# Block-diagonal q laid out in pairs of heads: two-word runs in the score matmuls' moving operand and 512-byte runs in its loads

## The chip, the cores and the metric

The kernel runs on one core of a Trainium2 chip. The metric is the device time of one execution in microseconds (us), lower is better. Engines are named as the profile names them: PE is TensorE (PEld its weight loads), DVE VectorE, ACT ScalarE, POOL GpSimd, SP SyncE, which here only issues DMAs. A "q" behind a name (SPq, ACTq) is that engine's sequencer issuing a DMA.

## What is computed

One decoder layer with three sub-layers, each followed by a residual add and a layer norm, on x of 16 x 256 tokens x 512. The change lies in the first one, a differential attention *across the heads of one token*:

```
q = split(x @ Wq.T) * SCALE      # per token 32 half-heads of 16 dims
k = split(x @ Wk.T)              # the same shape
v = x @ Wv.T                     # per token 16 heads of 32 dims
att  = softmax(q k^T)            # per token
diff = att[:, :16, :16] - lam * att[:, 16:, 16:]
out  = rmsnorm(diff @ v) * (1 - LAM_INIT)
x = layernorm(x + out @ Wo.T + bo)
```

The other two sub-layers are a decayed running sum of ctx*ctx multiplied onto x, and a feed-forward net with ternary weights (512 to 2048 to 512, squared relu). All of it is in float32 precision; large products are made of three (projections) or two (feed-forward) float32r matmuls of a high and a low part.

## The kernel before, in words

The 4096 tokens are cut into 8 blocks of 512 (`NSB`, `SB`). Phase A (`phase_a`, some 455 us) does projections, scores, softmax and the mix with v, in a software pipeline: body(i) of every engine holds the projections of block i, the scores and softmax of block i-1 and the mix of block i-2. Bodies 2 to 5 run in a hardware loop of two bodies per turn. Phase B (`phase_b`) does the rest, block after block; the last block's softmax and mix ("late") are spread over it. Everything is ordered by hand with semaphores; each engine runs its instructions strictly in program order.

In body(i) PE does twelve projection chunks n = 0 to 11 (`project`, L603: 12 matmuls of 512 columns each): 0 to 3 are q, 4 to 7 are k, 8 to 11 are v. Between them it does four bursts of scores of block i-1 (`scores`, L620) behind chunks 0, 1, 6 and 8 (`AT_SCORES`), four bursts of the mix of block i-2 (`mix`, L639) behind chunks 3 to 6 (`AT_MIX`), and four small sums for the ternary weights (`w_sums`, L677).

A token's scores are a product of 16 x 32 by 16 x 32. Eight tokens (`LANES`) share one matmul: lane t keeps its 16 dims on partitions 16t to 16t+15, and the moving operand `qbd` is block-diagonal, zero outside lane t's own slot. The stationary operand is `k2[:, :, g]` (32 columns), and the moving operand is

```
qbd = sb("y", "qbd", [P, LANES, H, G], F32)                       # before, L147
k2[:, :, g], qbd[:, :, :, g].rearrange("p a b -> p (a b)")        # L622
```

so its 128 columns are single words, G = 64 words (256 bytes) apart. Four such matmuls, for four column quarters of the array (32 outputs each), run side by side. Each float32 matmul is two instructions in the trace, so a burst of 32 matmuls shows as x64. The mix has the same construction and the same stride in its stationary operand (`v2[:, :, ...]`, 64 words), but its moving operand `dbd[:, :, n, :]` is eight runs of 16 neighbouring words; a burst of 16 matmuls shows as x32.

How q gets there: ACT copies each projection chunk from the PSUM bank `ps_f` into one of three buffers of `f_sb` (`f_copy`, L902 for q and k, L904 for v), first waiting for the DMA that emptied that buffer, and then issues a DMA into the scratch tensor `q_scr`, `k_scr` or `v_scr` (L909, L911). PE's chunk n waits for ACT's copy of chunk n-2. SP issues the loads: `first_half_load(i)` (k2 and the eight lanes of q for scores bursts 0 and 1), `second_half_load(i)` (the eight lanes of q for bursts 2 and 3), all of them through `q_load` (L388). SP's order in body(i) is: load of x, `dbd_load(i-2)` (L418, eight DMAs that place the softmax difference block-diagonally), `w_write(i-1, 1)`, `w_load(i, 0)`, `second_half_load(i-1)`, `v2_load(i-1)` (L400), `w_write(i, 0)`, `w_load(i, 1)`, `first_half_load(i)`, `o_write(i-2)`.

ACT's order in body(i): `f_copy` 0 to 11; `exps` 0 to 3 (L917, the softmax exponentials of block i-1) behind copies 1, 3, 8 and 11; `w_abs` and `w_sign` (L930, L934) behind copy 2, which wait for the weight load; `mixed` (L923) behind copies 4, 5 and 6 (twice); four `x_upper` (L887) behind copy 7.

DVE's order in body(i): `soft_first` 0 and 1 (L1109 to L1122: transpose out of PSUM, clean, subtract the maximum), `mixed_turn` 0 (L1230), `soft_second` 0 (L1132 on, which waits for the exponentials), `mixed_turn` 1, `square_sum` 0 (L1235), `w_signs`, `soft_second` 1, `mixed_turn` 2, `square_sum` 1, `w_signs`, `mixed_turn` 3, `square_sum` 2 and 3, `rms_seed`, `soft_first` 2, `soft_second` 2, four `x_lower` (L1082), `soft_first` 3, `w_signs`, `soft_second` 3, `diff_turn` (L1221, releases `dbd_load`), `w_signs`.

## Time and profile before

| | |
|---|---|
| runs | 1107.18, 1110.10, 1112.32 us; median 1110.1 us |
| the profiled execution | 1117.94 us, of which the span of its instructions is 1115.8 us |
| PE busy | 1045.4 us (94%), mean granted clock 0.971 |
| DVE, ACT, POOL busy | 868.6, 567.8, 274.4 us |
| DMA | 140.48 MB in 167466 packets, 140368 of them under 512 bytes |
| phase A / the seam / phase B | until about 455 us / 455 to 530 us / from 530 us on |

Busy time counts a matmul from its start to its modelled end; matmuls overlap, so the pace of a burst has to be read from its length and count, not from the mean of one. "PEclk" is the granted clock of PE as a share of 2.4 GHz (0.50 is 1.2 GHz). A bracket behind a line of a timeline, [1.57 <-DMA ...], is the time for which the engine stood idle before it, and what released it.

### The profile page before, as it was taken

The page shows a single profiled execution, that of the slowest core. Times are in us where ns is not written, and L with a number is a line of the kernel's source. Part 1 is how long each engine was busy: PE and PEld are TensorE (multiplying, and loading weights), DVE is VectorE, ACT ScalarE, POOL GpSimd, SP SyncE. Part 2 cuts the span into 40 slices and gives each one's busy share as a digit, 9 for nine tenths or more (in the row PEclk, how much of TensorE's full clock was granted, in tenths as well). Part 3 has the DMA queues.
Part 4 walks back from the last instruction along what each step waited for, and adds up shares of the span by engine and source line. Part 5 has one row for each costly group of instructions (what it writes and reads, how often), then busy time and mean ns, then how long its engine had stood idle before and what let it go on. Part 6 is the DMA issues. An engine that isn't in the chain of part 4 may idle for free.

```text
span 1115.8 us, 19236 instructions
## 1 busy us (share of the span) xinstructions
PE 1045.4 (94%) x6992; PEld 825.1 (74%) x7008; DVE 868.6 (78%) x1326; ACT 567.8 (51%) x866; POOL 274.4 (25%) x272
## 2 busy tenths in 40 slices
PE   6999899899999999686999999999999999999996
PEld 5777667677667776564788888888888888888885
DVE  4478888888889897788798988858958868587455
ACT  5423433334343424323567576665765766656673
POOL 5322252515252525226002003020022320200001
PEclk9999999999999998886999999999999999999998
DMA  7897595958778786978220223411403303110011
GB/s 283 245 225 186 133 242 134 234 150 188 204 162 226 170 249 128 252 189 327 38 76 1 76 76 62 114 43 32 129 1 76 114 1 81 71 38 1 1 38 38
DMA packets 167466, 140.48 MB, mean 126 GB/s; under 512 B 140368, under 2 KB 140880, under 8 KB 161488
## 3 DMA queue, kind: packets, MB, share of 16 engines
q1 hardware_dynamic: 96080, 113.83, 36.9%
q10 hardware_dynamic: 71296, 25.43, 9.3%
q8 instruction: 58, 0.95, 0.4%
q14 instruction: 32, 0.26, 0.1%
HBM read 82.61 MB, written 52.95 MB: 121 GB/s over the span
## 4 chain that ended last, share of the span: by engine, by line
PE 68%; DVE 13%; ACT 5%; DMA 5%; issue 4%; SPq 3%; ACTq 1%; POOL 0%; DVEq 0%; POOLq 0%
PE ps_s L792 20%; PE ps_f L776 19%; PE ps_f L603 12%; PE ps_o L728 7%; PE ps_s L620 5%; SPq L418 2%; DMA w_in<-in_fc_turned 2%; DVE row_sum L1132 1%; PE ps_o L639 1%; DMA w_scr<-w_in 1%; DVE o_sb L1230 1%; ACT f_sb L902 1%; DVE st L1145 1%; DMA w_raw<-in_qkvo 1%; PE ps_t L762 1%
## 5 line engine op out<-in xcount | busy, mean ns | idle before, releaser
L776 PE MATMUL ps_f<-x2h,w 128*128 128x512 f32 x512 | 205.0, 400 | 2.7 <-DVE x2l L1374 2.7
L776 PE MATMUL ps_f<-x2l,w 128*128 128x512 f32 x512 | 201.1, 393 | 0.0
L792 PE MATMUL ps_s<-w,hh 128*128 128x512 f32 x500 | 196.6, 393 | 0.0
L792 PE MATMUL ps_s<-w,hl 128*128 128x512 f32 x500 | 194.9, 390 | 0.0
L1382 DVE TENSOR_TENSOR hl<-h_sb,hh 128x512 fp32r<-128x512 f32 x128 | 90.0, 703 | 100.7 <-ACT hh L1004 100.6
L603 PE MATMUL ps_f<-xth,wh 128*128 128x512 f32 x376 | 158.2, 421 | 8.7 <-ACT f_sb L902 5.6
L603 PE MATMUL ps_f<-xtl,wh 128*128 128x512 f32 x376 | 149.6, 398 | 0.0
L603 PE MATMUL ps_f<-xth,wl 128*128 128x512 f32 x376 | 149.4, 397 | 0.0
L620 PE MATMUL ps_s<-qbd,k 128*32 128x128 f32 x2048 | 124.9, 411 | 11.7 <-DMA qbd<-q_scr 11.7
L994 ACT ACTIVATE r_sb<-ps_f 128x512 f32<-128x512 f32 x128 | 75.7, 591 | 104.7 <-PE ps_f L776 104.5
L620 PEld LDWEIGHTS ps_s<-qbd,k 128*32 128x32 f32 x2048 | 82.6, 147 | 49.1 <-issue 12.1
L776 PEld LDWEIGHTS ps_f<-x2h,w 128*128 128x128 f32 x512 | 97.3, 190 | 23.2 <-issue 3.6
L776 PEld LDWEIGHTS ps_f<-x2l,w 128*128 128x128 f32 x512 | 97.2, 190 | 19.4
L1574 POOL TENSOR_TENSOR w_in<-w_in,gscale 128x512 f32<-128x512 f32 x32 | 52.8, 1651 | 231.7 <-DVE gscale L1257 216.7
L792 PEld LDWEIGHTS ps_s<-w,hh 128*128 128x128 f32 x500 | 93.9, 188 | 19.1
L792 PEld LDWEIGHTS ps_s<-w,hl 128*128 128x128 f32 x500 | 94.0, 188 | 18.9
L1603 POOL TENSOR_TENSOR ln_rs<-ln_x,neg_half 128x4 f32<-128x4 f32 x23 | 23.2, 1009 | 338.0 <-DVE ln_x L1329 338.0
L1012 ACT ACTIVATE h_sq<-h_sb 128x512 f32<-128x512 f32 x128 | 79.4, 620 | 52.3 <-DVE h_acc L1393 52.2
L603 PEld LDWEIGHTS ps_f<-xth,wh 128*128 128x128 f32 x376 | 72.4, 192 | 34.8 <-issue 15.9
L902 ACT ACTIVATE f_sb<-ps_f 128x512 f32<-128x512 f32 x64 | 38.3, 599 | 112.8 <-PE ps_f L603 102.5
L603 PEld LDWEIGHTS ps_f<-xth,wl 128*128 128x128 f32 x376 | 72.4, 193 | 16.2
L1004 ACT ACTIVATE hh<-h_sb 128x512 fp32r<-128x512 f32 x128 | 81.0, 633 | 4.1
(158 smaller groups left out, 1832.1 us busy)
## 6 DMA issues: line engine op xcount, KB each, us to landing
q_scr<-f_sb ACTq DMA_DIRECT2D x32, 256.0 KB, 4.3
k_scr<-f_sb ACTq DMA_DIRECT2D x32, 256.0 KB, 2.6
w_scr<-w_in SPq DMA_DIRECT2D x16, 512.0 KB, 4.0
k<-k_scr SPq DMA_DIRECT2D x8, 1024.0 KB, 8.8
qbd<-q_scr SPq DMA_DIRECT2D x128, 64.0 KB, 4.6
v_scr<-f_sb ACTq DMA_DIRECT2D x32, 256.0 KB, 6.1
cx<-in_ctx_turned SPq DMA_DIRECT2D x8, 1024.0 KB, 4.9
xb<-in_x SPq DMA_DIRECT2D x8, 1024.0 KB, 5.2
```

What stands on the lines that cost most here:

```text
L603: last = nc.tensor.matmul(ps_f[:, n % 2, :], w[:, n // 4, k, cols], xx[:, par, k, :], start=(k == 0 and xx is xth and w is wh), stop=(k == ...
L620: last = nc.tensor.matmul(ps_s[32 * j:32 * (j + 1), 2 * (c % 2) + gq // 4, (gq % 4) * P:(gq % 4 + 1) * P], k2[:, :, g], qbd[:, :, :, g].re ...
L728: last = nc.tensor.matmul(proj_bank(i, t), a[:, k, rows], w[:, k, :], start=(k == 0 and w is woh and a is oth), stop=(k == KC - 1 and a is ...
L776: last = nc.tensor.matmul(ps_f[:, j % 2, :], w1[:, j // 2, k, (j % 2) * P:(j % 2 + 1) * P], xx[:, k, :], start=(k == 0 and xx is x2h), sto ...
L792: last = nc.tensor.matmul(ps_s[:, t, :], a[:, j % 4, t * P:(t + 1) * P], w2[:, j, :], start=(j == 0 and a is hh), stop=(j == HC - 1 and a ...
L902: nc.scalar.activation(f_sb[:, n % 3, :], ps_f[:, n % 2, :], ACT.Copy).then_inc(f_ev, 1)
L994: nc.scalar.activation(r_sb[:], ps_f[:, j % 2, :], ACT.Relu).then_inc(r_done, 1)
L1004: nc.scalar.activation(hh[:, j % 4, :], h_sb[:, j % 4, :], ACT.Copy).then_inc(hh_done, 1)
L1012: nc.scalar.activation(h_sq[:, j % 2, :], h_sb[:, j % 4, :], ACT.Square).then_inc(hq_done, 1)
L1382: nc.vector.tensor_tensor(hl[:, j % 4, :], h_sb[:, j % 4, :], hh[:, j % 4, :].bitcast(F32), ALU.subtract).then_inc(hl_done, 1)
L1574: nc.gpsimd.tensor_tensor(w_in[:, half(r)], w_in[:, half(r)], gscale[:, half(r)], ALU.mult).then_inc(wt_md, 1)
L1603: nc.gpsimd.tensor_tensor(y[:], x[:], neg_half[:], ALU.pow).then_inc(signal, 1)
```

## The change

The columns of Wq are reordered on the host, so that chunks 0 and 1 hold the first half-head set with even and odd heads and chunks 2 and 3 the second. ACT writes an even chunk into every even word of a new buffer `q_sb` and an odd chunk into every odd word, so that two heads of one token are neighbours. One DMA per pair of chunks writes 4096 bytes per partition into `q_scr` (16 such DMAs of 512 KB in place of 32 of 256 KB), and `q_load` reads it back in runs of 128 words, 512 bytes (the eight DMAs of 64 KB each stay). `qbd` keeps its size and becomes [P, LANES, H/2, G, 2]: the score matmul's moving operand is now 64 pairs of neighbouring words, 512 bytes apart. `f_sb` gets a fourth buffer (q_sb lies over it), with the waits rewritten for that. `o_sq` now lies over `dt`, and `r_sb` and three regions move in SBUF. Number and sizes of matmuls, ACT and DVE instructions stay.

```
-    q_scr = nc.dram_tensor("q_scr", [NSB, D, SB], F32, kind="Internal").ap()
+    q_scr = nc.dram_tensor("q_scr", [NSB, 2, P, LANES, 2 * G], F32, kind="Internal").ap()
+        q_sb = sb("x", "q_sb", [P, 2, SB, 2], F32)
-        f_sb = sb("x", "f_sb", [P, 3, SB], F32)
+        f_sb = sb("x", "f_sb", [P, 4, SB], F32)
-        qbd = sb("y", "qbd", [P, LANES, H, G], F32)
+        qbd = sb("y", "qbd", [P, LANES, H // 2, G, 2], F32)
...
             def q_load(i, s):
                 for t in range(LANES):
-                    sp.dma_start(qbd[H * t:H * (t + 1), lane_slot(t), :, :],
-                                 q_scr[i, s * 256:(s + 1) * 256, t * G:(t + 1) * G]
-                                 .rearrange("(d a) g -> d a g", a=H)).then_inc(qbd_ld, 16)
+                    sp.dma_start(qbd[H * t:H * (t + 1), lane_slot(t), :, :, :].rearrange("p a g r -> p a (g r)"),
+                                 q_scr[i, s, :, t, :].rearrange("(d a) n -> d a n", a=H // 2)).then_inc(qbd_ld, 16)
...
-                                            k2[:, :, g], qbd[:, :, :, g].rearrange("p a b -> p (a b)"),
+                                            k2[:, :, g], qbd[:, :, :, g, :].rearrange("p l a r -> p (l a) r"),
...
             def f_copy(i, n):
                 act.wait_ge(f_ps, at(i, 12, n + 1))
-                if n >= 3 or later(i):
-                    act.wait_ge(f_wr[n % 3], at(i, 64, 16 * (n // 3)))
+                if n < 4 and n % 2 == 0 and later(i):
+                    act.wait_ge(f_wr[n], at(i, 48, 0))
+                    act.wait_ge(f_wr[n + 1], at(i, 32, 0))
+                if 4 <= n < 8 and n % 2 == 0:
+                    act.wait_ge(f_wr[n % 4], at(i, 48, 16))
+                if n >= 8:
+                    act.wait_ge(f_wr[n % 4], at(i, 48 - 16 * (n % 2), 32 - 16 * (n % 2)))
...
+                if n < 4:
+                    nc.scalar.activation(q_sb[:, n // 2, :, n % 2], ps_f[:, n % 2, :], ACT.Copy).then_inc(f_ev, 1)
...
+                if n in (0, 2):
+                    return
                 act.wait_ge(f_ev, at(i, 12, n + 1))
                 if n < 4:
-                    act.dma_start(q_scr[i, rows, :], f_sb[:, n % 3, :]).then_inc(f_wr[n % 3], 16)
+                    act.dma_start(q_scr[i, n // 2].rearrange("p t n -> p (t n)"),
+                                  q_sb[:, n // 2, :, :].rearrange("p n r -> p (n r)")).then_inc(f_wr[n - 1], 16)
```

## Rows read from the trace of the kernel before

**Rows 1.** Busy time by stretch: us, each engine's busy (instructions), PEclk, DMA, GB/s.
```profile
core 0: us, PE busy (x) PEld busy (x) DVE busy (x) ACT busy (x) POOL busy (x), PEclk, DMA share, GB/s
254.20:313.40 59.20, 54.54 (x538) 40.74 (x534) 52.15 (x62) 22.43 (x29) 22.84 (x25) 1.00 0.78 190
530.00:1116.00 586.00, 572.18 (x2755) 471.48 (x2753) 437.31 (x802) 374.04 (x612) 76.69 (x72) 0.99 0.19 53
```

**Rows 2.** The chain that ended last: shares of the span by line.
```profile
by line: PE ps_s L792 19.9%; PE ps_f L776 19.4%; PE ps_f L603 11.6%; PE ps_o L728 6.5%; PE ps_s L620 5.4%; issue 4.4%; SPq L418 2.2%; DMA w_in<-in_fc_turned 1.7%; DVE row_sum L1132 1.5%; PE ps_o L639 1.3%; DMA w_scr<-w_in 1.2%; DVE o_sb L12
```

**Rows 3.** PE's timeline, 258 to 320 us: start, length, instruction, count, [idle before].
```profile
280.57 3.92 PE L620 MATMUL ps_s<-qbd,k 128*32 128x128 f32 x64 [1.57 <-DMA qbd<-q_scr]
...
296.89 1.11 PE L639 MATMUL ps_o<-dbd,v 128*32 128x128 f32 x32
...
312.28 1.11 PE L639 MATMUL ps_o<-dbd,v 128*32 128x128 f32 x32 [1.47 <-DVE o_sb L1230]
```

**Rows 4.** One instruction of the scores and of the mix: ns minimum/median/maximum, first and last.
```profile
L620 PE MATMUL ps_s<-qbd,k x2048: 393/413/440, 51.4 to 498.9; 128*32 128x128 f32 x187
...
L639 PE MATMUL ps_o<-dbd,v x896: 272/273/429, 117.7 to 475.5; 128*32 128x128 f32 x180
```

**Rows 5.** PE's timeline around the seam, and the granted clock there.
```profile
457.95 7.61 PE L620 MATMUL ps_s<-qbd,k 128*32 128x128 f32 x128 [4.03 <-DMA qbd<-q_scr]
466.07 1.11 PE L639 MATMUL ps_o<-dbd,v 128*32 128x128 f32 x32 [0.52 <-DMA dbd<-dt]
...
473.99 1.94 PE L639 MATMUL ps_o<-dbd,v 128*32 128x128 f32 x32 [1.29 <-DVE o_sb L1230]
...
459.00:462.00 3.00, 3.00 (x60) 2.17 (x56) 2.74 (x4) 0.00 (x0) 0.79 (x1) 0.75 0.32 73
474.00:477.00 3.00, 1.93 (x32) 1.35 (x32) 3.00 (x3) 2.66 (x5) 0.00 (x0) 0.50 1.03 317
```

**Rows 6.** The chain from 193 to 314 us: start, length, what.
```profile
254.22 3.69 PE ps_s L620 x57
...
266.63 1.23 DVE row_sum L1132
...
284.59 1.26 DVE dt L1221
...
292.63 2.85 DMA w_scr<-w_in
...
295.71 4.16 DMA w_in<-in_fc_turned
```

**Rows 7.** Who waited for whom (us in total, times, longest); DVE's timeline at 443 us.
```profile
DVE row_sum L1132 <- ACT sc L917: 13.9, 8, 2.3
...
DVE st L1109 <- PE ps_s L620: 11.4, 5, 4.0
...
443.52 1.22 DVE L1132 TENSOR_REDUCE row_sum<-sc 128x32 f32<-128x1024 f32 x1 [1.25 <-ACT sc L917]
```

**Rows 8.** The chain from 30 to 136 us: the first q load, four projection chunks.
```profile
45.61 5.76 DMA qbd<-q_scr
...
62.12 11.38 PE ps_f L603 x48
```

**Rows 9.** ACT's timeline in the first pipelined block.
```profile
66.18 1.06 ACT L930 ACTIVATE w_b<-w_in 128x1024 bf16<-128x1024 f32 x1 [0.47 <-DMA w_in<-in_fc_turned]
...
68.24 0.57 ACT L902 ACTIVATE f_sb<-ps_f 128x512 f32<-128x512 f32 x1
```

**Rows 10.** ACT's groups by shape: busy, mean ns of one, idle before.
```profile
L923 ACT ACTIVATE o_sq<-o_sb 128x512 f32<-128x512 f32 x28 | 31.0, 1106 | 36.8 <-DVE o_ms L1235 17.9 <-DVE o_sb L1230 12.3 <-ACT f_sb L902 6.6
L904 ACT ACTIVATE f_sb<-ps_f 128x512 f32<-128x512 f32 x32 | 19.2, 601 | 43.5 <-PE ps_f L603 42.4 <-DMA v_scr<-f_sb 1.1
```

**Rows 11.** A pause of PE with a lower clock behind it: timeline, and stretch.
```profile
339.76 3.92 PE L620 MATMUL ps_s<-qbd,k 128*32 128x128 f32 x64 [1.57 <-DMA qbd<-q_scr]
...
342.00:345.00 3.00, 3.00 (x36) 2.10 (x29) 2.77 (x4) 0.00 (x0) 0.14 (x1) 0.60 0.99 381
```

More of the change, by code:

```diff
@@ L91, in program @@
         base = (nc.sbuf_base + 31) // 32 * 32
-        region = {"x": base, "y": base + 90 * 1024, "z": base + 122 * 1024,
-                  "c": base + 154 * 1024, "s": base + 202 * 1024}
+        region = {"x": base, "y": base + 92 * 1024, "z": base + 124 * 1024,
+                  "c": base + 156 * 1024, "s": base + 202 * 1024}
         spot = dict(region)
@@ L153, in program @@
         p1 = sb("c", "p1", [P, G, H], F32)
+        o_sb = sb("c", "o_sb", [P, HD, G], F32)
+        spot_c = spot["c"]
+        o_sq = sb("c", "o_sq", [P, SB], F32)
+        spot["c"] = spot_c
         dt = sb("c", "dt", [P, G, H], F32)
-        o_sb = sb("c", "o_sb", [P, HD, G], F32)
-        o_sq = sb("c", "o_sq", [P, SB], F32)
         w_b = sb("c", "w_b", [P, 2 * D], BF16)
@@ L218, in program @@
         f_ps, f_ev = sem("f_ps"), sem("f_ev")
-        f_wr = [sem(f"f_wr{n}") for n in range(3)]
+        f_wr = [sem(f"f_wr{n}") for n in range(4)]
         qbd_ld = sem("qbd_ld")
@@ L380, in hold, with q_written, k_written, v_written @@
                     sp.sem_inc(passed, 1)
-            def f_written(i, chunks):
-                return [(f_wr[n % 3], at(i, 64, 16 * (n // 3 + 1))) for n in chunks]
+            def q_written(i, s):
+                return [(f_wr[2 * s], at(i, 48, 16))]
+            def k_written(i):
+                return [(f_wr[n], at(i, 48 - 16 * (n % 2), 32 - 16 * (n % 2))) for n in range(4)]
+            def v_written(i):
+                return [(f_wr[n], at(i, 48 - 16 * (n % 2), 48 - 16 * (n % 2))) for n in range(4)]
             def q_load(i, s):
                 for t in range(LANES):
-                    sp.dma_start(qbd[H * t:H * (t + 1), lane_slot(t), :, :],
-                                 q_scr[i, s * 256:(s + 1) * 256, t * G:(t + 1) * G]
-                                 .rearrange("(d a) g -> d a g", a=H)).then_inc(qbd_ld, 16)
+                    sp.dma_start(qbd[H * t:H * (t + 1), lane_slot(t), :, :, :].rearrange("p a g r -> p a (g r)"),
+                                 q_scr[i, s, :, t, :].rearrange("(d a) n -> d a n", a=H // 2)).then_inc(qbd_ld, 16)
             def k2_load(i):
@@ L979, in x2_upper @@
                 if t == 0 and not later(i):
-                    for n in range(3):
-                        act.wait_ge(f_wr[n], at(NSB, 64, 0))
+                    for n in range(4):
+                        act.wait_ge(f_wr[n], at(NSB, 48 - 16 * (n % 2), 0))
                     act.wait_ge(wt_wr, at(NSB, 32, 0))
@@ L1656, in turned, with q_columns, k_columns @@
     return a.reshape(NSB, SB, KC, P).transpose(0, 3, 2, 1)
-def head_columns(w, order):
-    return w.T.reshape(D, H, QD, 2).transpose(0, *order).reshape(D, D)
+def q_columns(w):
+    return w.T.reshape(D, H // 2, 2, QD, 2).transpose(0, 4, 2, 3, 1).reshape(D, D)
+def k_columns(w):
+    return w.T.reshape(D, H, QD, 2).transpose(0, 2, 3, 1).reshape(D, D)
 def layouts(inputs):
-    qkvo = np.stack([head_columns(inputs["L0_attn_Wq"], (3, 2, 1)), head_columns(inputs["L0_attn_Wk"], (2, 3, 1)),
+    qkvo = np.stack([q_columns(inputs["L0_attn_Wq"]), k_columns(inputs["L0_attn_Wk"]),
                      inputs["L0_attn_Wv"].T, inputs["L0_attn_Wo"].T])
```

22 lines of the change are left out of this document (12 added, 10 removed).

## The prediction, made before the changed kernel had run

> **What bounds the kernel now.** I read the busy time by stretch first. From 530 us to the end, more than half of the span, PE is busy 572 of 586 us and the change touches nothing there [rows 1]. In phase A it is less clear: a block takes about 59 us, PE is busy 54.5 and DVE 52.2 of 59.2 [rows 1]. So two engines are nearly full, and what is taken from one may leave the other. The chain of work that ended last gives the score bursts 5.4% of the span, 60.3 us or 16 of the 32 bursts [rows 2]. That is the most the matmul part of the change can touch. The same chain within a block then shows what closes the round: score burst 2 (254.22), projection, the exponentials, DVE's row_sum (266.63), DVE's dt (284.59), eight DMA issues of `dbd_load`, the write of ternary weights (292.63), the next weight load (295.71), ACT, DVE, and burst 2 again at 313.39 [rows 6]. Only one of the block's four bursts is in that round; the other three sit beside DVE work.
>
> **The change, part by part.**
>
> *The score matmuls.* A burst of 64 instructions takes 3.92 us [rows 3]; less the last one's own 0.41 [rows 4] and over 63 intervals that is 55.7 ns each. The mix has the same 128 columns, the same 32 output columns and the same stride of its stationary operand, but runs of 16 words in the moving one: 1.11 us for 32 [rows 3], less 0.27 [rows 4], over 31: 27 ns. So reading single words 256 bytes apart costs half the rate. The clock confirms it: in the seam two bursts in a row take 7.61 us, (7.61 - 0.41) / 127 = 56.7 ns, though the granted clock was down to 0.75 there, while a mix burst at 0.50 takes 1.94 us, (1.94 - 0.43) / 31 = 49 ns [rows 4, 5]. The scores keep one pace at both levels of the clock (1.2 and 2.4 GHz), and it is about the mix's pace at the lower one; the mix follows the clock. A fetch of one word at a time at a fixed rate would explain both, and two words per fetch would just feed the upper level. No row shows runs of two words. The bounds are 55.7 ns (no gain) and 27 ns; I take 27, since the factor to be closed is two and the run length is two. A burst then takes 2.05 us in place of 3.92, 1.87 less at full clock and nothing at half clock.
> The Trainium skill ("Advanced Engine Details and Errata", SBUF Cachelines) says that SBUF is read in lines of 16 bytes and that at least two hits on a line are needed to absorb the access latency. By that rule two words get the full rate, as above, and the sum is this one; the trace agrees with it for one word (55.7 ns) and for sixteen (27), and no row tries two.
>
> *What of it counts.* Twice 1.87 before burst 2 of the first block, where PE alone is in the chain. But ACT cannot do copy 3 before the weight load lands: it starts at 68.24, behind two operations that began at 66.18 when the load came [rows 9]. Four chunks took 11.38 us, 2.85 each, and ended at 73.50 [rows 8]. Projection 5 waits for that copy: 68.24 + 0.6 + 2.85 = 71.7 against 73.5, so 1.8 is gained there, not 3.7; burst 2's own 1.87 then reaches DVE, which was waiting for it. Sum 3.7.
> From then on the round of rows 6 decides. DVE's row_sum waited 13.9 us in 8 cases for the exponentials [rows 7], because ACT took projection copies 7 and 8 first, and these waited for PE. PE 1.87 earlier frees ACT, but an exponential takes 1.1 itself and can't begin before DVE's own subtraction; where it did begin at once the wait was 1.25 [rows 7]. So seven waits fall to 1.25: 13.4 - 8.8 = 4.6. The eighth (0.53, last block) gives 0.5. DVE also waited 11.4 us in 5 cases directly for scores [rows 7]; 8.6 of it lies in the start already counted, 2.8 in one block after a long pause of PE; 0 to 2.8, I take 1.1, since the weight load is late next. These make 6.2.
> The other bursts are faster beside DVE work: nothing. PE will arrive earlier at burst 0 and wait longer for the q load.
>
> *The loads.* Half of the packets of the q loads go; their eight issues per half stay. The load is in the chain once, 5.76 us at the start [rows 8]; between nothing and a third of it (q is a third of the bytes landing with k2): 0 to 1.9, I take 0.5. Elsewhere PE waits 1.57 for it without being the bound [rows 3].
> The Trainium skill ("DMA: Bandwidth & Descriptors", Why small descriptors are slow) gives a 256-byte descriptor 11 cycles, which makes a 512-byte one 19 by the same formula: 14% less per byte, near the low end; no row here separates the q loads' packets.
>
> *The writes.* 32 DMAs of 256 KB become 16 of 512 KB. The one behind copy 2 was issued beside the weight load of rows 6 (4.16 us) and is now gone; 256 KB at the 317 GB/s seen in a full stretch [rows 5] are 0.8 us. 0 to 0.8 in each of six blocks; I take 0.3: 1.8. The pair's write lands later, but the q loads wait for the k chunks, written afterwards. The new waits are as loose as the old: copy 4 waits for a write issued behind copy 1, three chunks back as before. SP's extra waits are for semaphores long reached. Behind ACT's wait at copy 2 stand `w_abs` and the rest of ACT; it is for v writes of the block before, as it was.
>
> *ACT's strided copies.* Output in every second word, 32 times. Nearest rows: 601 ns for a copy with a permuted output in 16-word runs, and 1106 ns for a square that reads words 256 bytes apart [rows 10]. I take 600, since two neighbouring hits in 16 bytes are the closer case, so nothing. At 1106 only copy 3 lies in the round (weights, copy 3, exponential, copy 4, square, DVE): 0.5 x 6 = 3.0 lost.
>
> *What comes late next.* In the seam PE had scores to do from 457.95 to 465.6; now it is through about 2 to 3.7 us earlier and pauses before the mix at 466.07, which runs in the chain at full clock (1.11), where the third and fourth take 1.94 at half clock [rows 5]. I count two at the lower clock: 2 x 0.83 = 1.7 lost.
>
> Sum: 3.7 + 4.6 + 0.5 + 1.1 + 0.5 + 1.8 - 1.7 = 10.5 us. Against the profiled execution's own 1117.9 (span 1115.8 and 2.1 around it) that gives 1107.4; the median of the runs is 7.8 lower, 1110.1, and the saving, which is phase A's and not a share of the whole, is the same there: **1099.6 us**.
>
> **The rivals.**
>
> *Two words aren't enough.* The matmuls stay at 56 ns, the change doesn't do its main work, and the loads and writes remain: 0.5 + 1.8, or less 3.0 if the copies are slow. 1107.8 to 1110.8, say 1108. For it: no row has such runs. Against it: the fixed pace at both clocks, which looks like one word per fetch. 21%.
>
> *The chain's share in full.* PE was the real bound throughout, and other waits follow it down: 60.3 us of bursts in the chain times 1.87 / 3.92 are 28.8 us less, 1081. Against it: DVE's 52.2 busy of 59.2, plus the waits for exponentials that can't go. 13%, with anything beyond 1088.
>
> *The clock takes it back (slower).* PE now has 10 us or more of pauses per block. The pause before the fourth mix is 1.47 us [rows 3], and a pause of 1.57 elsewhere was followed by a clock of 0.60 [rows 11], one of 1.57 at 280.57 by none. If pauses before that mix grow or add up so that the clock is 0.50 behind it, burst 2 gains nothing and projections 7 and 8, 2.85 us each at full clock [rows 8], take twice that: 5.7 us late in a round that has no slack for it. In all five steady blocks: 28.5 lost and the 4.6 not won; with the rest of the sum, 1110.1 - 5.9 + 28.5 = 1132.7. Each such block costs 5.7 and 0.7 of the gain, so one or two leave a small gain or none, and from three on it is slower. Against it: nothing before that mix gets faster, since no score burst lies between chunk 2 and it. The skill's "TensorE: Matmul & The Clock Gate" (HAM oscillation) warns of just this, full clock lost again after waits; the trace agrees after the pause in rows 11 and not after the one in rows 3. 10%.
>
> **How the numbers follow.** The forecast's own case, 1092 to 1106, has 56%. The four cases make 100%. The range reaches to the "not enough" case and its slow copies above, and to half of the full share below: 1086 to 1113; outside it are most of the full-share case and the clock case, and some of the main one. A measurement of this kernel can tell about 0.5%, 5.6 us, from no change. Faster: nearly all of the main case, all of the full share: 68%. Same: "not enough", and edges of the main and the clock case: 23%. Slower: 9%.
>
> **What the profile of the changed kernel would show.** The score burst: x64 in about 2.05 us in full clock (3.9 would mean that pairs don't help; 3.0 that they help by half). ACT's q copies at 0.60. The row_sum wait of burst 2 at about 1.25. A block of about 58 us with PE busy near 50. The pause before burst 0, behind the q load, at 5 us in place of 1.57, with a lower clock behind it that harms nobody. In the seam mix bursts of 1.94. Wrong would be the forecast if blocks fell to 55 us (then PE was the bound), or if the clock were at 0.5 in the projections behind burst 2.

## The result, and the profile after

The changed kernel takes 1107.1 us against 1110.2 us for the kernel before on the same chip (20 runs each): ratio 0.9971, 95% interval 0.996 to 0.9981, so 2.1 to 4.4 us less, 3.2 by the ratio. The forecast was 10.5 less. Direction right, size three times too large. The profiled execution has a span of 1106.2 us; single executions scatter by some 5 us, so its 9.6 us to the profile of before are not the result.

First the page of the changed kernel, the lines that answer to the table shown of before:

```profile
span 1106.2 us, 19193 instructions
PE 1017.5 (92%) x7008; PEld 824.6 (75%) x7008; DVE 876.5 (79%) x1326; ACT 570.4 (52%) x866; POOL 278.9 (25%) x272
...
PEclk9999999999999989686999999999999999999998
...
DMA packets 148777, 140.47 MB, mean 127 GB/s; under 512 B 107344, under 2 KB 124240, under 8 KB 142800
```

PE has 28 us less to do and the span of this profile is down by 9.6: most of what PE saved turned into waits of PE. Note DVE: its work is the same, instruction for instruction, and it is busy 7.9 us longer. That is the first sign of where the rest went. The same in one block (us, busy of each engine with its count, clock, DMA share, GB/s):

```profile
133.00:192.00 59.00, 50.97 (x533) 40.50 (x532) 53.59 (x61) 22.11 (x29) 23.02 (x24) 0.97 0.72 187
```

PE 50.97 against 54.54 in [rows 1], DVE 53.59 against 52.15.

Next the score matmuls: PE's timeline, and the instruction's own time (ns minimum/median/maximum):

```profile
315.76 2.57 PE L632 MATMUL ps_s<-qbd,k 128*32 128x128 f32 x64
```

```profile
L632 PE MATMUL ps_s<-qbd,k x2048: 297/312/441, 48.1 to 489.0; 128*32 128x128 f32 x187
```

Where [rows 3] had 3.92 us there are now 2.57 to 2.63: (2.57 - 0.31) / 63 = 35.9 ns each, where 27 were forecast. Of the 1.87 us forecast for a burst, 1.3 came.

The waits that answer to [rows 7] (who waited for whom, us in total, times, longest), and two that grew:

```profile
DVE row_sum L1153 <- ACT sc L938: 9.1, 7, 2.3
...
ACT w_b L951 <- DMA w_in<-in_proj_turned: 15.0, 6, 3.1
...
PE ps_f L615 <- ACT q_sb L918: 7.8, 8, 2.0
```

The wait for the exponentials fell from 13.9 us in 8 cases to 9.1 in 7: 1.13 us in each but the first. That step went as forecast. ACT now waits in six blocks for the other half of the weight load (15.0 us in all; 0.6 and 1.7 in the two executions of the kernel before), and PE waits a little longer for the copies of q (7.8 us against 5.6). What stands behind row_sum in the same block did not go as forecast. Here are DVE and POOL from chunk 2's subtraction (L1122, L1143 in the changed kernel) on, first in a second execution of the kernel before (start, length, instruction, [idle before]):

```profile
201.29 1.32 DVE L1122 SCALAR_TENSOR_TENSOR sc<-sc,row_max 128x1024 f32<-128x1024 f32 x1
203.68 2.62 POOL L1565 TENSOR_TENSOR o_sb<-o_sb,o_rs 128x512 f32<-128x512 f32 x2
204.65 1.22 DVE L1132 TENSOR_REDUCE row_sum<-sc 128x32 f32<-128x1024 f32 x1 [2.04 <-ACT sc L917]
205.90 0.35 DVE L1135 RECIPROCAL row_inv<-row_sum 128x32 f32<-128x32 f32 x1
206.29 0.75 DVE L1145 SCALAR_TENSOR_TENSOR st<-sc,lam,row_inv 128x512 f32<-128x512 f32 x1
```

and then in the changed kernel:

```profile
138.96 1.60 DVE L1143 SCALAR_TENSOR_TENSOR sc<-sc,row_max 128x1024 f32<-128x1024 f32 x1
141.69 1.22 DVE L1153 TENSOR_REDUCE row_sum<-sc 128x32 f32<-128x1024 f32 x1 [1.12 <-ACT sc L938]
141.81 2.54 POOL L1586 TENSOR_TENSOR o_sb<-o_sb,o_rs 128x512 f32<-128x512 f32 x2 [0.26 <-POOL o_rs L1579]
142.94 0.35 DVE L1156 RECIPROCAL row_inv<-row_sum 128x32 f32<-128x32 f32 x1
143.33 1.56 DVE L1166 SCALAR_TENSOR_TENSOR st<-sc,lam,row_inv 128x512 f32<-128x512 f32 x1
```

POOL's two multiplies (the rms scaling of the block before) started 0.97 us ahead of row_sum and ended at 206.30, just as DVE's `scalar_tensor_tensor` began at 206.29: they ran in DVE's wait and beside a reduction. In the changed kernel the multiplies start 0.12 us behind row_sum, and the same DVE instruction takes 1.56 us in place of 0.75. Counted from burst 2 and block for block, row_sum comes 0.6 us sooner and the multiplies 0.3 us later (at 7.39 to 7.59 us in place of 7.13 to 7.33), since POOL's small steps ahead of them take longer. The subtraction ahead of the exponential has grown too, from 1.32 to 1.60. The subtraction of chunk 3 meets the second pair of multiplies in both kernels: 2.17 to 2.21 us in the kernel before, 2.17 to 2.51 in the changed one.

The kernel before shows the meeting once itself, in its last block, where row_sum had waited only 1.25 us. From its first execution, block 2 and the last one:

```profile
205.24 2.62 POOL L1565 TENSOR_TENSOR o_sb<-o_sb,o_rs 128x512 f32<-128x512 f32 x2
207.86 0.75 DVE L1145 SCALAR_TENSOR_TENSOR st<-sc,lam,row_inv 128x512 f32<-128x512 f32 x1
...
443.37 2.61 POOL L1565 TENSOR_TENSOR o_sb<-o_sb,o_rs 128x512 f32<-128x512 f32 x2
445.17 1.36 DVE L1145 SCALAR_TENSOR_TENSOR st<-sc,lam,row_inv 128x512 f32<-128x512 f32 x1
```

Where the time went, by stretch, in us. All numbers are read from DVE's and PE's timelines; "burst 2" is DVE's transpose of burst 2. Of the columns of numbers the third and fourth are means of five blocks, the fifth of six.

| execution | first burst to burst 2, first block | six blocks | burst 2 to row_sum | row_sum to dt | dt to the next burst 2 | last burst 2 to the end |
|---|---|---|---|---|---|---|
| before, first and second | 29.08, 29.27 | 355.7, 354.1 | 8.02, 8.04 | 17.83, 17.82 | 33.6, 33.3 | 679.6, 680.2 |
| after, first and second | 27.71, 25.46 | 352.2, 351.4 | 7.46, 7.41 | 18.81, 18.81 | 32.6, 32.5 | 678.1, 679.2 |

In the two middle columns, where the forecast had its largest term, a block got 0.6 us shorter and 1.0 longer. These two repeat to 0.05 us. The others hold landings of DMAs and scatter, so that the two pairs differ by 9.6 and 6.7 us in all, where the runs give 3.2.

### The profile page after: what moved, and what is told of

Read it like the earlier page. It is cut to its first block, busy times and chain, and to the rows that moved or that the text cites. A ratio compares the mean times of both kernels' runs of the same rounds, so it can differ in the third digit from the quotient of the medians.

```text
span 1106.2 us, 19193 instructions
## 1 busy us (share of the span) xinstructions
PE 1017.5 (92%) x7008; PEld 824.6 (75%) x7008; DVE 876.5 (79%) x1326; ACT 570.4 (52%) x866; POOL 278.9 (25%) x272
## 4 chain that ended last, share of the span: by engine, by line
PE 54%; DVE 24%; ACT 6%; issue 6%; DMA 4%; SPq 3%; ACTq 2%; POOL 0%; DVEq 0%; POOLq 0%
PE ps_s L804 20%; PE ps_f L788 20%; PE ps_o L740 6%; SPq L430 3%; PE ps_f L615 3%; DVE row_sum L1153 2%; DMA w_in<-in_fc_turned 2%; DVE st L1166 2%; DVE sc L1136 2%; DVE row_max L1139 2%; DVE st L1130 2%; DMA w_scr<-w_in 2%; ACT o_sq L944 1%; ACTq L932 1%; DVE gscale L1278 1%
## 5 line engine op out<-in xcount | busy, mean ns | idle before, releaser
L1595 POOL TENSOR_TENSOR w_in<-w_in,gscale 128x512 f32<-128x512 f32 x32 | 56.0, 1751 | 220.0 <-DVE gscale L1278 206.2
L632 PE MATMUL ps_s<-qbd,k 128*32 128x128 f32 x2048 | 84.3, 322 | 7.5 <-DMA qbd<-q_scr 7.5
L632 PEld LDWEIGHTS ps_s<-qbd,k 128*32 128x32 f32 x2048 | 74.9, 139 | 16.9 <-DMA qbd<-q_scr 8.8
L615 PEld LDWEIGHTS ps_f<-xtl,wh 128*128 128x128 f32 x376 | 73.4, 195 | 14.3
```

Source lines behind the costliest of these rows:

```text
L615: last = nc.tensor.matmul(ps_f[:, n % 2, :], w[:, n // 4, k, cols], xx[:, par, k, :], start=(k == 0 and xx is xth and w is wh), stop=(k == ...
L632: last = nc.tensor.matmul(ps_s[32 * j:32 * (j + 1), 2 * (c % 2) + gq // 4, (gq % 4) * P:(gq % 4 + 1) * P], k2[:, :, g], qbd[:, :, :, g, :] ...
L1595: nc.gpsimd.tensor_tensor(w_in[:, half(r)], w_in[:, half(r)], gscale[:, half(r)], ALU.mult).then_inc(wt_md, 1)
```

## The experiments

Each ratio is to runs of the kernel before on the same chip, with its 95% interval; "us" is the ratio's difference times 1111. Bursts are those of the first block.

### The two kernels once more

> The kernel before once more, for a second profile of it. The first one took 1117.9 us while the runs lie at 1110.2, and the gap between the two profiles (spans 1115.8 and 1106.2, 9.6 us) is three times the measured gain of 3.1. Theory A (the first profile was an unusual execution): this one is at 1108 to 1113, with steady blocks of 57.5 to 59.5 us, without the load of 6.07 us and the PE stall that made two blocks 60.5 long. Theory B (profiling costs this kernel 7 us): it is at 1117 again with the same blocks.

> The changed kernel once more. Its blocks should repeat: about 58.5 us each, score bursts of 2.6 us, DVE's L1166 behind the exponentials of burst 2 at about 1.56 us, where L1145 of the kernel before takes 0.75, if that is the regular collision with POOL's multiplies that I take it for; at 0.75 in half of the blocks if it is chance.

Measured: 1113.7 and 1107.0 us, spans 1111.5 and 1104.9, so theory A within a microsecond. In both executions of the kernel before the `scalar_tensor_tensor` of chunk 2 takes 0.75 to 0.89 us in every block but the last, which has 1.36; in the changed kernel it takes 1.38 to 1.56 from the second block on (in the second execution from the third). So the pattern belongs to the kernels, not to one execution.

### Pair reads alone, and words in place of pairs

```
-  k2[:, :, g], qbd[:, :, :, g].rearrange("p a b -> p (a b)"),              # before
+  k2[:, :, g], qbd[:, :, 0:16:2, 2 * (g // 2):2 * (g // 2) + 2],            # e1
-  ... qbd[:, :, :, g, :].rearrange("p l a r -> p (l a) r"),                 # after
+  ... qbd[:, :, :, g, :].rearrange("p l a r -> p l r a"),                   # e2
```

> The kernel before with only the score matmuls' moving operand changed: 64 pairs of neighbouring words, 512 bytes apart, from the old layout, so it multiplies wrong columns of q; loads, copies and writes are those of before. Theory 1 (the matmuls' reads are the whole effect, and DVE's round decides): bursts of 2.6 us and a time like the changed kernel's, 1106 to 1108.5. Theory 2 (matmuls bring more, and the strided copies of 0.69 us and the larger writes take it back): 1101 to 1104.

> The changed kernel with the moving operand read in an order that makes every word single again (512 bytes apart; heads come out permuted), so only loads, copies, writes and buffers are changed. Bursts of 3.9 us. Theory 1: 1109.5 to 1112, no difference from before. Theory 2: 1112 to 1116, the copies and writes cost.

Measured: e1 0.9938 (0.9918 to 0.9958), 6.9 us less, with bursts of 2.23 us. e2 1.0102 (1.008 to 1.0124), 11.3 us more, with bursts of 4.90 us:

```profile
47.56 4.90 PE L632 MATMUL ps_s<-qbd,k 128*32 128x128 f32 x64
```

Neither fits its theories: the time of e1 is in the range of theory 2, but its bursts are not the 2.6 us that both took for given, and e2 is above every range. Pairs alone gain twice what the whole change does; and single words cost 70 ns ((4.90 - 0.48) / 63) where the kernel before paid 55.7. So at the same run length the new layout is slower than the old, and something in the addresses beside the run length sets the pace. In both kernels four matmuls, for four column quarters ("tiles"), run side by side and read columns g that are 16 apart: 64 bytes in the kernel before and in e1, 128 in the changed kernel and in e2. (Against the kernel before, e2 also doubles the step within one matmul, from 256 to 512 bytes, so for single words the two are not separated. For pairs they are: the step is 512 bytes in all of the kernels with pairs.)

### Is it the rest of the change, or the addresses?

```
-  qbd[:, :, :, g, :]                                            # after
+  qbd[:, :, :, g // 2, :]                                       # e10
-  nc.scalar.activation(q_sb[:, n // 2, :, n % 2], ps_f...       # after
+  nc.scalar.activation(<q_sb[:, n // 2] as 1024 words>[(n % 2) * SB:(n % 2 + 1) * SB], ps_f...   # e7
```

> The changed kernel, but matmul g reads the pairs of column g // 2 instead of g (so the scores are made from other columns of q). Every matmul still reads 64 pairs of words 512 B apart; only the distance between the four column tiles' reads falls from 128 to 64 B, as it is in the kernel before with pair reads (bursts 2.23 us there, 2.6 us in the changed kernel). Theory 'address': the 2.6 us come from where the pairs lie; bursts fall to 2.2 to 2.3 us, the waits of chunk 2's row_sum stay at 1.13 us, the first block and the blocks' lengths hardly move, and the time is 0 to 1.5 us under the changed kernel (3 to 4.6 us under the kernel before). Theory 'rest of the change': bursts stay at 2.6 us and the time stays 3.1 us under the kernel before.

> The changed kernel, but each of the four copies of q writes 512 words in one run, each chunk in its own half of the paired buffer (so q's words are in another order). Theory 'strided copies': they cost 694 ns against 599 ns, 28 of them, and TensorE's projection waits for them; the copies fall to 600 ns, the waits of the projection for q_sb fall from 7.8 us by 1 to 2 us, and the time is 1.5 to 3 us under the changed kernel (4.6 to 6 us under the kernel before). Theory 'the copies are covered': they fall to 600 ns and the time stays within 0.7 us of the changed kernel.

Measured: e10 0.9931 (0.9908 to 0.9953), 7.7 less, bursts 2.23 us: with the addresses of e1 the changed kernel is as fast as e1 (0.8 us apart, give or take 3.3), so its copies, writes and loads together cost and bring nothing that shows. The theory 'address' was right on the bursts, and the time fell by more than the 3 to 4.6 us that I had put to it. e7 0.9972 (0.9957 to 0.9986), 3.1 less, the changed kernel's own time. ACT's group of q copies (busy, mean ns of one, idle before), first changed kernel, then e7:

```profile
L918 ACT ACTIVATE q_sb<-ps_f 128x512 f32<-128x512 f32 x32 | 22.1, 694 | 24.4 <-PE ps_f L615 20.7 <-DMA v_scr<-f_sb 3.0 <-PE ps_f L698 0.8
```

```profile
L918 ACT ACTIVATE q_sb<-ps_f 128x512 f32<-128x512 f32 x32 | 19.5, 609 | 35.8 <-PE ps_f L615 35.8
```

The strided copies cost 85 ns each and no time in all (0.1 us between e7 and the changed kernel, give or take 2). The second theory of e1, that they take the gain back, falls.

### Which property of the addresses?

```
-  qbd[:, :, :, g, :]      with g = j * 16 + (c % 2) * 8 + gq    # after: tiles 128 B apart
+  qbd[:, :, :, (c % 2) * 32 + j * 8 + gq, :]                    # e12: 64 B apart, no pair twice
+  qbd[:, :, :, 2 * (g // 2), :]                                 # e13: 128 B apart, each pair twice
+  qbd[:, :, :, (c % 2) * 32 + gq * 4 + j, :], copies permuted   # e14: 8 B apart
+  qbd[:, :, :, j * 16 + ((c + j) % 2) * 8 + gq, :]              # e19: 192 and 64 B apart in turn
```

> The changed kernel, but the matmul of row tile j, place gq reads the pair (c % 2) * 32 + j * 8 + gq instead of j * 16 + (c % 2) * 8 + gq (so other columns of q go into the scores). Each matmul still reads a pair of its own; the four tiles' reads lie 64 B apart instead of 128. Known: near pairs, each read twice and 64 B apart, gave bursts of 2.23 us and 7.9 us under the kernel before; the changed kernel 2.6 us and 3 us under it. Theory 'distance between the tiles': bursts 2.2 us, chunk 2's sc multiply-add at 1.35 us, time 6.5 to 8 us under the kernel before. Theory 'repeats' (the second matmul on the same pair is what was cheaper): bursts 2.6 us, that multiply-add 1.59 us, 3 to 4 us under the kernel before.

> The changed kernel, but matmul g reads pair 2 * (g // 2) (other columns of q): each pair is read by two matmuls in turn, and the tiles' reads stay 128 B apart. Theory 'distance between the tiles': bursts stay at 2.6 us, 3 to 4 us under the kernel before. Theory 'repeats': 2.2 us, 6.5 to 8 us under it.

> A whole kernel: the changed one with the copies of q permuted so that the column of row tile j, place gq is stored as pair (c % 2) * 32 + gq * 4 + j, and read there: the four tiles' reads lie 8 B apart, within 32 B. The copies read PSUM in a permuted order, so they may take over 694 ns; copies in a plain run changed no time. Theory 'distance between the tiles': bursts at most 2.2 us, possibly 1.8, and 6.5 to 10 us under the kernel before. Theory 'repeats': 2.6 us, 3 us under it. Should tiles that read within one 64-byte stretch get in each other's way, the bursts are over 2.6 us.

> The changed kernel, but row tiles 1 and 3 read the other half of their 16 columns (pair j * 16 + ((c + j) % 2) * 8 + gq, so other columns of q go into the scores): neighbouring tiles read 64 and 192 B apart in turn, in different 64-byte halves, and tiles two apart read 256 B apart, as in the changed kernel. Theory 'halves' (two reads collide when they lie in the same 64-byte half of 128 bytes): bursts 2.05 us and 6 to 9 us under the kernel before. Theory 'distance' (the four reads have to lie within 256 B): bursts 2.6 us and 3 us under it.

The kernel before with runs of 16 words asks what the floor is:

```
+  k2[:, :, g], qbd[:, :, 0, 16 * (g // 16):16 * (g // 16) + 16],            # e3, in before
```

> The kernel before with the moving operand of each score matmul read as 8 runs of 16 words (other columns of q). Theory 'pairs 64 B apart are at the floor': bursts 2.05 us, as with such pairs, and 7 to 10 us under the kernel before. Rival 'pairs still wait for SBUF': bursts 1.8 us or less. The tiles read 64 B apart here too.

| kernel | run, words | tiles apart | burst, us | ratio (interval) | us |
|---|---|---|---|---|---|
| before | 1 | 64 B | 3.92 | 1 | 0 |
| e2 | 1 | 128 B | 4.90 | 1.0102 (1.008 to 1.0124) | +11.3 |
| after | 2 | 128 B | 2.63 | 0.9971 (0.996 to 0.9981) | -3.2 |
| e13 | 2, each twice | 128 B | 2.61 | 0.9969 (0.9953 to 0.9986) | -3.4 |
| e19 | 2 | 192 and 64 B | 2.63 | 0.9963 (0.9949 to 0.9977) | -4.1 |
| e14 | 2 | 8 B | 2.61 | 0.998 (0.9962 to 0.9997) | -2.2 |
| e1 | 2, each twice | 64 B | 2.23 | 0.9938 (0.9918 to 0.9958) | -6.9 |
| e10 | 2, each twice | 64 B | 2.23 | 0.9931 (0.9908 to 0.9953) | -7.7 |
| e12 | 2 | 64 B | 2.07 | 0.9919 (0.9888 to 0.995) | -9.0 |
| e3 | 16, all of a tile the same | 64 B | 1.98 | 0.9921 (0.9892 to 0.9949) | -8.8 |

The rows of e12, e19 and e3 from PE's timelines:

```profile
52.38 2.03 PE L632 MATMUL ps_s<-qbd,k 128*32 128x128 f32 x64
```

```profile
49.20 2.63 PE L632 MATMUL ps_s<-qbd,k 128*32 128x128 f32 x64 [1.65 <-DMA qbd<-q_scr]
```

```profile
50.10 1.98 PE L620 MATMUL ps_s<-qbd,k 128*32 128x128 f32 x64 [1.65 <-DMA qbd<-q_scr]
```

With tiles 64 B apart a pair takes (2.03 - 0.27) / 63 = 27.9 ns, and 16 words 27.1: two words are enough, as forecast, if the four tiles' reads lie right. The mix's 27 ns [rows 3, 4], with other words for every matmul, say the same as e3. "Repeats" fall (e13), and so do "halves" (e19). Near isn't enough either (e14). The times follow the bursts: the three kernels with bursts of 2.6 and plain or strided copies (e7, e13, e19) and the changed one lie at 0.9963 to 0.9972, the four with 2.23 or less and e15 below at 0.9919 to 0.9938. Half a microsecond a burst goes with 4.4 us (means 0.9969 and 0.9929); with e14, left out here for its permuted copies, it would be 4.6.

More than half of this lies in DVE's stretches. In e1, e3, e10, e12 and e15 the two middle columns of the table are 7.18 to 7.22 and 18.46 to 18.60 us, in e7, e13, e19 and the changed kernel 7.41 to 7.47 and 18.74 to 18.81: half a microsecond in each of five blocks, 2.6 us. In the first column it is DVE's subtraction ahead of the exponential (L1143), 1.23 to 1.36 us in the first group and 1.44 to 1.62 in the second. In e14 that one is short and the reduction ahead of it is long; in e2, the other kernel with slow reads, it is row_sum:

```profile
199.23 1.47 DVE L1140 TENSOR_REDUCE row_max<-sc 128x32 f32<-128x1024 f32 x1
```

```profile
206.65 1.33 DVE L1153 TENSOR_REDUCE row_sum<-sc 128x32 f32<-128x1024 f32 x1 [2.51 <-ACT sc L938]
```

Both take 1.22 us in the kernel before. In all of these kernels the long instruction runs, at least in part, beside PE's burst 3. That slow reads of PE hold up DVE is not shown by this; no run separates it from POOL's work, which runs there too.

### The meeting of POOL and DVE

The four multiplies that end the rms scaling were cut to 8 of their 64 columns, in both kernels:

```
-  nc.gpsimd.tensor_tensor(o_tile(i)[:, rows, :], o_tile(i)[:, rows, :], o_rs...      # G = 64 columns
+  nc.gpsimd.tensor_tensor(o_tile(i)[:, rows, 0:8], o_tile(i)[:, rows, 0:8], o_rs[:, 0:8]...
```

> The kernel before with GpSimd's last multiply of the attention output (the rms scaling) on 8 of 64 columns, so 7/8 of that scaling is left out. It is the base for the next run. DVE's second scalar_tensor_tensor stays at 0.75 us. Theory 'contention takes the gain back': the multiply overlapped only a reduction here, so the time stays within 2 us of the kernel before (0 to -2 us). Rival 'the block is bound elsewhere': the same.

> The changed kernel with GpSimd's rms scaling on 8 of 64 columns (7/8 of it left out). In the changed kernel VectorE's second scalar_tensor_tensor took 1.39 to 1.57 us beside that multiply, against 0.75 us before, and the stretch from chunk 2's row_sum to the dt transpose grew by 1 us a block. Theory 'contention takes the gain back': without the multiply it is 0.75 us again, the stretch is back at 17.7 us, and the gain against the kernel before with the same cut is 8 to 10 us. Rival 'the gain is lost elsewhere' (strided copies, another wait): the gain between the two cut kernels stays at 3 to 4 us, whatever that instruction takes.

Measured: e5 0.996 (0.9946 to 0.9974), e6 0.9881 (0.9861 to 0.99). Between the two cut kernels the change is worth 0.9881 / 0.996 = 0.9921, 8.8 us, where it is worth 3.2 between the whole ones. With the intervals of both (root of the squared halves, 0.0024 for the first and 0.001 for the second), 5.6 us, give or take 2.9, are given back where POOL multiplies. The 8.8 are inside the 8 to 10 of the theory. In e6, DVE and POOL again:

```profile
140.33 1.22 DVE L1153 TENSOR_REDUCE row_sum<-sc 128x32 f32<-128x1024 f32 x1 [1.13 <-ACT sc L938]
140.44 0.60 POOL L1586 TENSOR_TENSOR o_sb<-o_sb,o_rs 128x64 f32<-128x64 f32 x2 [0.26 <-POOL o_rs L1579]
141.97 0.75 DVE L1166 SCALAR_TENSOR_TENSOR st<-sc,lam,row_inv 128x512 f32<-128x512 f32 x1
```

The stretch from row_sum to dt is 16.85 us in e5 and 17.10 in e6: the multiplies cost 1.0 us a block in the kernel before and 1.7 in the changed one. I had expected 0 to 2 us for e5; it was 4.4, since chunk 3's last `scalar_tensor_tensor` was slowed in the kernel before already (2.17 us, 1.23 here). The Trainium skill ("SBUF — State Buffer", Who interferes with whom) states that a VectorE instruction with two SBUF inputs contends with a GpSimd instruction that reads SBUF, its second input coming through a read interface that the two engines share, and that reductions on this chip never do. The traces agree: `row_sum` and `row_max` take 1.22 us in every case with a multiply beside them, in both kernels, while the two-input steps behind them take up to 0.8 us (chunk 2, 512 words) and 1.3 us (chunk 3, 1024 words) longer.

### Moving the multiplies instead of cutting them

The cut also makes POOL itself faster (0.4 us in place of 1.4 for a multiply), so by itself it does not single out the meeting. Moving the multiplies keeps POOL's work. Only the semaphores for which POOL waits ahead of its four multiplies change:

```
-  o_scale(i - 2, (s_sub, 3), (s_sub, 3), (s_add, 4), (s_add, 4))       # values within the block; the last block keeps its own
+  o_scale(i - 2, (s_sub, 3), (xt_lo), (s_add, 4), (wt_pn, 3))          # e8
+  o_scale(i - 2, (s_sub, 3), (xt_lo), (xt_lo), (s_add, 4))             # e18, e20
```

> The changed kernel with three of GpSimd's four rms scaling multiplies given other starting points in the block: the first after this block's sc steps as before, the second once the next block's projection input is there, the third after chunk 4's sum, the fourth at the weight step, so that none runs beside chunk 2's second scalar_tensor_tensor on VectorE. Theory 'contention takes the gain back': that instruction is 0.75 us in most blocks, and half or more of the 7 us that the cut multiply gave comes back: 6 to 9 us under the kernel before. Rival 'it only moves': another VectorE step on the chain, or the output of the block, is late instead, and the time is within 1.5 us of the changed kernel or above it.

> The changed kernel with other starting points for GpSimd's four scaling multiplies: the first beside the row_sum reduction, the second and third together once the next block's projection input is there (beside the transpose of st), the fourth beside the row_max reduction. The weight step's multiplies keep their place. Theory 'contention takes the gain back': chunk 2's scalar_tensor_tensor is 0.75 us and chunk 3's last multiply-add 1.23 us, the stretch from row_sum to dt falls from 18.8 to 17.4 to 17.9 us, and the time is 6 to 9 us under the kernel before. Rival 'it only moves': the stretch stays over 18.3 us and the time within 1.5 us of the changed kernel.

> The kernel before with GpSimd's four scaling multiplies at the other starting points (beside row_sum, two beside the transpose of st, one beside row_max). The changed kernel gained 3 us by it. In the kernel before chunk 2's scalar_tensor_tensor was at 0.75 us already and only chunk 3's last multiply-add (2.17 to 2.5 us) can fall to 1.23 us. Theory 'the pairs moved the meeting': it gains about half as much here, 0 to 2.5 us under the kernel before. Rival 'the same in both': 3 us or more.

Measured: e8 0.9979 (0.9964 to 0.9995), no gain over the changed kernel (0.9 us behind it, give or take 2.1). Chunk 2's instruction is at 0.75 us, but the fourth multiply pushed POOL's weight multiplies beside DVE's last two steps, which are on the way to dt:

```profile
210.62 1.30 POOL L1586 TENSOR_TENSOR o_sb<-o_sb,o_rs 128x512 f32<-128x512 f32 x1 [2.79 <-DVE w_b L1281]
211.88 1.57 POOL L1595 TENSOR_TENSOR w_in<-w_in,gscale 128x512 f32<-128x512 f32 x1
...
212.09 1.92 DVE L1166 SCALAR_TENSOR_TENSOR st<-sc,lam,row_inv 128x512 f32<-128x512 f32 x1
214.04 1.58 DVE L1170 TENSOR_TENSOR p<-p,st 128x512 f32<-128x512 f32 x1
```

That is the rival "it only moves", but only in part: in the five blocks row_sum to dt still fell to 18.30 us, half a microsecond under the changed kernel, and where that went is not shown. e18 has a place for all but one: 0.9939 (0.9915 to 0.9963), 6.8 us less than before and 3.6 less than the changed kernel, give or take 2.9, row_sum to dt at 18.03 us in place of 18.81. One meeting is left:

```profile
204.38 2.99 POOL L1586 TENSOR_TENSOR o_sb<-o_sb,o_rs 128x512 f32<-128x512 f32 x2 [4.62 <-DVE xtl L1103]
206.25 2.20 DVE L1136 SCALAR_TENSOR_TENSOR sc<-st,sc 128x1024 f32<-128x1024 f32 x1
```

The same move in the kernel before (e20) gives 1.0009 (0.9991 to 1.0028), 1.0 us more, give or take 2.1: nothing, as the theory "the pairs moved the meeting" had it (0 to 2.5 us), and not the 3 us or more of its rival. There it wins back chunk 3's second `scalar_tensor_tensor` and loses the first (2.20 us against 1.23), and chunk 2's was at 0.75 anyway; row_sum to dt stays at 17.85. So what the moved multiplies give in the changed kernel is, within these intervals, what the change had newly brought about.

### A whole kernel with both

Each q copy becomes two of 256 words, so that the tiles read 64 B apart; e17 adds the moved multiplies of e18.

```
+  for h in range(2):
+      last = nc.scalar.activation(
+          q_sb[:, n // 2, :, n % 2].rearrange("p (t h j q) -> p t h j q", t=LANES, h=2, j=4)[:, :, h],
+          ps_f[:, n % 2, :].rearrange("p (t j h q) -> p t j h q", t=LANES, j=4, h=2)[:, :, :, h], ACT.Copy)
+  last.then_inc(f_ev, 1)
...
+  k2[:, :, g], qbd[:, :, :, (c % 2) * 32 + j * 8 + gq, :].rearrange("p l a r -> p (l a) r"),
```

> A whole kernel: the changed one with each copy of q made as two copies of 256 words, so that the column of row tile j, place gq is stored as pair (c % 2) * 32 + j * 8 + gq, and read there: the four tiles read 64 B apart. With the same reads and the plain copies the time was 9 us under the kernel before (interval 5.6 to 12.4). Theory 'the tiles' addresses': bursts 2.05 us, chunk 2's sc multiply-add 1.33 us, time 6 to 9 us under the kernel before. Rival 'the copies': ScalarE has 8 steps more a block pair (two of some 400 ns for one of 694), TensorE's projection waits longer for q_sb (over 12 us in all), and the time is 0 to 4 us under the kernel before.

> Both in one whole kernel: q stored so that the four tiles read 64 B apart, and the scaling multiplies moved. If the two are separate causes, their gains add up: 10 to 15 us under the kernel before. If both lie on the same slack, the better of the two alone: 6 to 9 us.

Measured: e15 0.9938 (0.9914 to 0.9963), 6.9 less: bursts 2.07. It is 2.1 us behind e12, give or take 4.4, so a price of the doubled copies (411 ns each) does not show. e17 **0.9898** (0.9879 to 0.9917), 11.3 less, 1100.8 us against 1111.3: the fastest of all whole kernels, better than both the kernel before and the changed one. The two gains over the changed kernel, 3.7 and 3.6, add up to 7.3, and 8.1 were measured. With intervals of some 3 us on each, that fits two causes with a price of their own, as the expectation had it (10 to 15), and not one slack that both lie on (6 to 9).

## Why the prediction was wrong, step by step

*What bounds the kernel.* Right in its main line: PE and DVE share the bound, the chain's 5.4% was not to be had in full, and the rival at 1081 us fell. The warning "what is taken from one may leave the other" was written and not carried through to the sum. Two terms failed, both on something that stood beside the instruction that I was looking at.

*The pace of the pairs* is the first step that failed. The term was 1.87 us a burst and measured 1.3. "Two words per fetch would just feed the upper level" was right for tiles that read 64 B apart (27.9 ns in e12). I had looked at the stride within one matmul alone. That the change also moves the four tiles' reads from 64 to 128 B apart stood in the layout, and the experiments price it at 4.4 us. My bounds for a pair, 27 and 55.7 ns, held; I took the end and not a value between. The Trainium skill states that at least two hits on a 16-byte line of SBUF are needed to absorb the access latency ("Advanced Engine Details and Errata", SBUF Cachelines); I had taken two for enough, and the trace agrees only for tiles that read 64 B apart: the changed kernel has two hits and 35.9 ns.

*The stall that goes* is the second. Seven waits were to fall to 1.25 us, worth 4.6 us; they fell to 1.13. But between burst 2 and row_sum a block got only 0.6 shorter, since chunk 2's `scalar_tensor_tensor` ahead of the exponential (L1143) went from 1.32 to 1.59 us, and the stretch behind row_sum got 1.0 longer. Net, the two stretches got 0.4 us longer a block, where they were to get 0.65 shorter: in five blocks 2 us lost, where 3.3 were to be won. The question was what is late next; I answered with an engine's own work and its floor, and not with what another engine had been doing in that wait. The rows for it were in the trace of before: POOL's multiplies at 205.24, ending as DVE's instruction began at 207.86, and, two rows behind the very wait of 1.25 us that I had taken for the floor [rows 7], the same instruction at 445.17 with 1.36 us in place of 0.75. No rival of mine had this.

*The first block* came out about as forecast: 3.7 forecast; 29.27 to 25.46 in the second pair of executions, 3.8. In the first pair it was 1.4; the other kernels with 2.6 us bursts have 25.5 to 26.1 there, e14 apart (29.3).

*The block after PE's pause and the write behind copy 2* (1.1 + 1.8) stand together in the stretch from dt to the next burst 2, which got 0.8 to 1.0 us shorter on the mean of six blocks, 4.9 to 6 us where 2.9 were forecast. The shorter burst 2 is not the cause: from the second block on DVE's transpose of burst 2 begins with no idle time before it in both kernels, 0.7 us behind the burst's end in the kernel before and 2.2 in the changed one. Nor is it clear that the write is: over all profiles the stretch has 32.7 to 33.6 us (mean 33.1) in the six with the old writes and 32.1 to 33.3 (mean 32.8) in the fourteen with the new. The 0.3 us a block between the means are what I had taken for the write, and less than the scatter.

*ACT's strided copies:* 694 ns, between the bounds 600 and 1106 and near the lower one, as taken; worth nothing (e7). *The loads:* half a microsecond was taken for the start; the landing's median went from 4.6 to 4.5 us. The first burst began at 48.12 us against 51.41 before, but in the second pair at 48.82 against 47.97, so nothing shows. e10 against e1 says that loads, writes and copies together are worth 0.8 us, give or take 3.3.

*The seam:* two more mix bursts at half clock were forecast, and all four have it. PE's timeline of the changed kernel:

```profile
448.75 6.56 PE L632 MATMUL ps_s<-qbd,k 128*32 128x128 f32 x128 [4.78 <-DMA qbd<-q_scr]
457.44 1.94 PE L651 MATMUL ps_o<-dbd,v 128*32 128x128 f32 x32 [2.13 <-DMA dbd<-dt]
460.62 1.94 PE L651 MATMUL ps_o<-dbd,v 128*32 128x128 f32 x32 [1.24 <-DVE o_sb L1251]
```

The score bursts now follow the clock: with 0.50 and 0.67 granted over 449 to 455 us, (6.56 - 0.44) / 127 = 48 ns, the mix's pace at the lower level. Against the 7.61 us of [rows 5] the two bursts gained 1.05 us there, where I had said "nothing at half clock"; two bursts at full clock gain 2.6. The 1.7 us that I took off for the seam don't show in the time: counted from DVE's transpose of the last burst 2, the fourth mix ends 1.2 to 2.2 us later than before, but the next projection, which waits for the load of Wo, starts at 41.86 and 42.19 us, against 41.86 and 41.80 before. The rival "the clock takes it back" fell: the block shown above had 0.97, and until the seam no slice of the page's PEclk is under 0.8.

So the sum, in the size that the runs give: the addresses take about 4.4 us and the meeting about 5.6, each priced alone. Without the meeting the change is worth 8.8 us, with bursts of 2.6 still (e6 over e5). If the two prices add, it would be worth 3.2 + 4.4 + 5.6 = 13.2 us with neither, more than the 10.5 forecast; that is an estimate, no run leaves out both. The forecast was too large because it had neither of these losses.

What stays open: why 64 B is right and 8, 128 and the mix of 64 and 192 B are not; and why chunk 2's L1143 takes 1.44 to 1.62 us in the kernels with 2.6 us bursts (in e14 the reduction ahead of it is long instead) and 1.23 to 1.36 in all others, with or without the long multiplies. It runs beside POOL's small steps of the root and beside PE's burst 3; neither was tried by itself. e14 is 1 us or more slower than the changed kernel, e13 and e19, but within the intervals; its permuted copies took 715 ns, and whether that is the cause was not tried either.

## What to carry to other kernels

Before counting a wait as gained, look at what every other engine does during it, and ask where that work lands once the wait is gone; a two-input VectorE step behind the wait and a GpSimd multiply inside it are a pair to look for. When the layout of a matmul's moving operand changes, check not only its run length but how far apart the reads of the column tiles lie that run beside it. And GpSimd work that has slack is best started beside reductions, which kept their time here, but a place has to be found for every piece: e8 moved three of four well and gained nothing that shows.

## What the hardware showed that I had not expected

- Float32 matmuls in four column tiles, 128 columns each, moving operand at a fixed stride, ns for each of the two instructions of a matmul: single words 55.7 with a stride of 256 B and tiles 64 B apart (before), 70 with 512 B and 128 B (e2); pairs, 512 B apart, 27.9 with tiles 64 B apart (e12) and 36 at 8 B (e14), 128 B (changed kernel, e13) and 192 and 64 B in turn (e19); 27.1 for runs of 16 words (e3). Two matmuls in a row on the same pair, 64 B apart: 30.8 ns ((2.23 - 0.29) / 63, e1 and e10).
- With single words 256 B apart the pace did not follow the clock (55.7 ns at full, 56.7 with 0.75 granted); with pairs it did (36 ns at full, 48 with 0.50 and 0.67 granted).
- A VectorE `scalar_tensor_tensor` of 512 words a partition took 0.75 us with no GpSimd multiply beside it and 1.36 to 1.75 with one that ran on beside it (chunk 2; the 1.75 is a single block of e1); one of 1024 words 1.23 and 2.17 to 2.51 (chunk 3). Reductions beside such a multiply stayed at 1.22.
- A ScalarE copy of 512 words took 694 ns on the mean with every second word as output (changed kernel) and 609 ns with one run as output (e7); 256 words, every second word as output, took 411 ns (e15).
